# Attention for pairs of query tiles: products of 256 columns, the value matrix applied to the result, rows of scores in 18 places, four gather buffers

## The reference, cut to what matters

```python
x = x + deformable_conv(groupnorm(x), offset_w, offset_b, conv_w)   # 8 images, 128 channels, 56 x 56
t = tokens(x)                                                       # 8 x 3136 x 128
n = layernorm(t)
q, k, v = n @ Wq.T, n @ Wk.T, n @ Wv.T
scores = where(causal, q @ k.T * 128 ** -0.5, -inf)
t = t + softmax(scores) @ v
m = layernorm(t)
probs = softmax(m @ gate_w.T + gate_b, over tokens)                 # 64 experts, top 8 tokens of each
t = t + scatter(experts(gather(m, top 8)), top 8)                   # gelu(pooled @ w1) @ w2 for 64 experts
```

## Time and profile before

| | us |
|---|---|
| median of 3 runs (3008.95 to 3011.6) | 3009.99 |
| the profiled execution | 3008.08 |
| its span, first to last instruction | 3006.3 |
| first part | 0 to 2813 |
| second part | 2813 to 3006 |
| one image in the steady part (1029.6 to 1364.0) | 334.5 |

### The profile page before, as it was taken

One profiled execution on the slowest core, in us unless ns is written; L12 is line 12 of the kernel. 1 busy time (PEld: TensorE's weight loads), 2 busy tenths in 40 slices (PEclk: granted clock), 3 DMA queues, 4 the chain that ended last, 5 costly groups with the idle time before them and its releaser, 6 DMA issues. The chain is left out here.

```text
span 3006.3 us, 52942 instructions
## 1 busy us (share of the span) xinstructions
PE 2696.6 (90%) x18970; PEld 2111.6 (70%) x18970; DVE 1896.5 (63%) x7132; ACT 1775.2 (59%) x4046; POOL 1752.8 (58%) x1813
## 2 busy tenths in 40 slices
PE   5788999999999999999999999999999998999555
PEld 3566776778777777778777776778777886777333
DVE  3566666766587667766587667766586658654314
ACT  2555666666666666666666666666666666664210
POOL 5777775775477656775577647775577657700000
PEclk8899999999999999999999999999999998999677
DMA  7444334633355325532354325532363324320497
GB/s 184 122 142 136 113 107 124 162 113 90 89 154 139 96 80 146 147 113 85 103 151 133 96 77 149 148 112 85 107 174 114 101 81 118 115 94 9 161 347 282
DMA packets 221233, 383.21 MB, mean 127 GB/s; under 512 B 44569, under 2 KB 131545, under 8 KB 220459
## 3 DMA queue, kind: packets, MB, share of 16 engines
q0 software_dynamic: 86400, 236.04, 27.5%
q1 hardware_dynamic: 130411, 128.81, 14.0%
q10 hardware_dynamic: 4160, 14.98, 1.2%
HBM read 317.04 MB, written 62.65 MB: 126 GB/s over the span
## 5 line engine op out<-in xcount | busy, mean ns | idle before, releaser
L521 POOL DMA_INDIRECT shared<-pair_table,idx x1800 | 1741.0, 967 | 882.5 <-issue 525.2
L1107 PE MATMUL bank_o<-vals,prob_t 128*128 128x128 f32 x5200 | 676.3, 277 | 73.3 <-ACT prob_t L566 72.4
L810 DVE CUSTOM_DVE_ANT_0 prob<-bank_r,mask 128x512 f32<-128x512 f32 (+3 forms) x728 | 452.0, 631 | 409.1 <-PE bank_r L1085 407.3
L1107 PEld LDWEIGHTS bank_o<-vals,prob_t 128*128 128x128 f32 x5200 | 622.1, 192 | 105.7 <-ACT prob_t L566 96.3
L566 ACT ACTIVATE prob_t<-bank_r 128x512 f32<-128x512 f32 (+3 forms) x728 | 383.0, 547 | 473.6 <-PE bank_r L1094 472.7
L1085 PE MATMUL bank_r<-keys,qt 128*128 128x512 f32 (+3 forms) x1456 | 633.7, 551 | 0.0
L547 ACT ACTIVATE shared<-shared,wa 128x128 f32<-128x128 f32 x1800 | 561.3, 391 | 38.6 <-DMA shared<-pair_table,idx 38.6
L800 DVE SCALAR_TENSOR_TENSOR shared<-shared,wb 128x128 f32<-128x128 f32 x1800 | 510.8, 347 | 84.8 <-ACT shared L547 83.0
L1074 PE MATMUL bank_r<-convw_t,smp_t 128*128 128x128 f32 x3600 | 485.8, 282 | 31.6 <-ACT smp_t L552 31.6
L1074 PEld LDWEIGHTS bank_r<-convw_t,smp_t 128*128 128x128 f32 x3600 | 449.8, 197 | 90.2 <-ACT smp_t L552 58.0
L1094 PE MATMUL bank_r<-ident,prob 128*128 128x128 f32 x2600 | 383.6, 274 | 1.9 <-ACT prob L639 1.9
(11 more groups left out here) (152 smaller groups left out, 2189.3 us busy)
## 6 DMA issues: line engine op xcount, KB each, us to landing
shared<-in_dram SPq DMA_DIRECT2D x32, 1024.0 KB, 10.0
shared<-pair_table,idx POOLq DMA_INDIRECT x1800
pair_table<-rows_out SPq DMA_DIRECT2D x112, 256.0 KB, 3.1
t<-in_dram SPq DMA_DIRECT2D x48, 256.0 KB, 3.6
t_dram<-t SPq DMA_DIRECT2D x48, 256.0 KB, 2.4
shared<-in_dram SPq DMA_DIRECT2D x7, 1568.0 KB, 14.3
stage<-t_dram SPq DMA_DIRECT2D x8, 832.0 KB, 9.8
pm_dram<-logit SPq DMA_DIRECT2D x8, 800.0 KB, 9.8
```

The lines of the kernel that those rows point to most:

```text
L521: pool.indirect_dma_start(g[t % RING][:, n, :], None, pair_table[b % 2], bass.IndirectOffsetOnAxis(ap=idx[:, b % 2, i * TAPS + n:i * TAPS ...
L810: dve.tensor_tensor_reduce(prob_at(t, k0, w), ring_bank(("score", t, c))[:, 0:w], m, 1.0, NEG, ALU.add, ALU.max, cmax[t % 2][:, c:c + 1]). ...
L1107: last = pe.matmul(attn_ps, prob_t[q % 3][:, n * P:(n + 1) * P], vals[:, slot(tb, at), :], start=(at == 0), stop=(at == ti))
```

## The change

**Pairs.** Attention is done for two query tiles at a time (`pair_tiles`, 13 pairs in an image, the last one of a single tile). The product is the other way round: a block of `vals` is the stationary side and the turned probabilities of both tiles are the moving one, 256 columns (L1238 of the new file); where only the second tile of the pair reaches a block, 128. `bank_o` then holds channels by tokens for the pair.

**The value matrix.** `vals` keeps the normalised tokens. After the last product of a pair DVE copies `bank_o` to `z` (L971, 128 x 256) and PE multiplies it by `wv_t` (`values`, L1249, one product for each tile) into a bank of the six. The odd jobs "vals" are gone. `t2` of both tiles is made in the one step in which the pair is finished (`tiles_done`): DVE's list for that step is the copy to `z`, three score banks, the layer norm for `vals` where due, `t2` and statistics twice, the layer norm for `xf` where due, the convolution's sum.

**Lags.** The exponential stays at 7 (`LAG_E`), the products start at 8 (`LAG_V`) and take two steps, the first half of a pair's pieces in one and the second half in the next (`attending`). The pair is finished one step later. In the rounds the scores now stand ahead of the products. The table of odd jobs, the top 8 (now steps 9 to 12) and the indices (13 to 18) are moved by about a step.

**Places.** `RING` is 4; what the fifth buffer took, and `prob`, make 18 places of 512 scores. A row may lie in one to three runs; then the exponential takes one to three instructions (247 for 200 tiles) and DVE adds the sums. DVE waits with a score for the turning of what lay in its place.

**Second part.** Stage pieces (L1370, L1382) are issued by POOL, behind waits of their own. SP issues w1 of round k + 2 behind `first(k - 2)`, and w2 of round k behind `second(k - 4)`; `first` waits for w1 alone and `second` for w2. Round 3's matrices are loaded at step 208 instead of 201.

```diff
-RING = 5
+RING = 4
-LAG_S, LAG_V, LAG_T = 6, 7, 8
+LAG_S, LAG_E, LAG_V = 6, 7, 8
-LMAX, LEXP, LTOP, LREPLACE, LCHOSEN, POOLED_OUT = 8, 9, 9, 10, 11, 15
-INDEX = (12, 13, 14, 16, 17)
+LMAX, LEXP, LTOP, LREPLACE, LCHOSEN, POOLED_OUT = 9, 10, 10, 11, 12, 16
+INDEX = (13, 14, 15, 17, 18)
+def pieces_of(p):
+    if len(pair_tiles(p)) == 1:
+        return [(k, min(PER, TILES - k)) for k in range(0, TILES, PER)]
+    return [(2 * j, 2) for j in range(p + 1)]
+def attending(step):
+    b, r = divmod(step - LAG_V, TILES)
...
+    return [(PAIRS * b + p, j) for j in (range(n // 2) if h == 0 else range(n // 2, n))]
+def finished(step):
+    b, r = divmod(step - LAG_V - 1, TILES)
+    if not 0 <= b < B or not (r % 2 or r == TILES - 1):
+        return None
+    return PAIRS * b + r // 2
@@ ACT
-                    act.activation(row, row, ACT.Exp, bias=nmax[r][:, 0:1], accum_out=total[r][:, 0:1])
+                    for k, (c0, w) in enumerate(runs):
+                        row = columns(c0, w)
+                        last = act.activation(row, row, ACT.Exp, bias=nmax[v % 2][:, 0:1],
+                                              accum_out=total[:, v % 4, k:k + 1])
-                early = chunks_in(v) >= 4
+                early = len(at) >= 4
@@ DVE
+                if pair is not None:
+                    w = len(pair_tiles(pair % PAIRS)) * P
+                    after(attended, pair + 1)
+                    after(valued, pair)
+                    dve.tensor_copy(z[:, 0:w], bank_o[:, 0:w]).then_inc(z_done, 1)
+                for c in range(min(chunks_in(ts), 3)):
+                    keep_scores(ts, c)
...
+                for h, t in enumerate(tiles_done(step)):
...
+                    after(valued, pair + 1)
...
+                    dve.scalar_tensor_tensor(t2[k % 2][:, j, :], ring_bank(("attn", pair, 0))[:, h * P:(h + 1) * P],
@@ PE
+                def values():
+                    use = ("attn", pair, 0)
+                    after(z_done, pair + 1)
+                    free_ring(use)
+                    for h in range(len(pair_tiles(pair % PAIRS))):
+                        last = pe.matmul(ring_bank(use)[:, h * P:(h + 1) * P], z[:, h * P:(h + 1) * P], wv_t[:],
                 for c in range(min(chunks_in(ts), 3)):
                     scores(c)
+                if pair is not None:
+                    values()
@@ second part, SP
-                if k >= WSLOTS:
-                    sp.wait_ge(second_mm, k - WSLOTS + 1)
-                    load_experts(sp, k, 1, w1, w2, shared, w_in)
+                if WSLOTS <= k + 2 < ROUNDS:
+                    sp.wait_ge(first_mm, k + 2 - WSLOTS + 1)
+                    load_experts(sp, k + 2, 1, w1, w2, shared, w_in)
```

More of the change, by code:

```diff
@@ L165, in ring_order @@
         order += [("score", ts, c) for c in range(min(chunks_in(ts), 3))]
+        if finished(step) is not None:
+            order.append(("attn", finished(step), 0))
         order += [("rows", *k) for k in rows_of(step)]
@@ L450, in _ @@
                 b, s = image_of(step)
-                t = step - LAG_T
-                if 0 <= t < ALL:
+                for t in tiles_done(step):
                     tb, i = image_of(t)
@@ L876, in _ @@
+                for t in [t for t in tiles_done(step) if t % TILES % PER == PER - 1 or t % TILES == TILES - 1]:
                     tb, i = image_of(t)
                     m, k = i % PER + 1, GPI * tb + i // PER
-                    at, first = k % 2 * PER, slot(tb, i - m + 1)
+                    row, first = k % 2 * PER, slot(tb, i - m + 1)
                     after(stats_b, t + 1)
@@ L1001, in fill_misc @@
                         last = pe.transpose(bank_misc[:, k * P:(k + 1) * P], vals[:, at + k, :], ident[:])
[L1002 to L1006 removed]
                 elif what == "query":
                     w = group_size(n) * P
+                    emptied(after, ("keys", b, n))
                     last = pe.matmul(bank_misc[:, 0:w], wqk[:], key_chunk(b, n * CHUNK, w), start=True, stop=True)
@@ L1056, in _ @@
             for step in range(END):
-                ts, v = step - LAG_S, step - LAG_V
+                ts, pair, at = step - LAG_S, finished(step), attending(step)
                 b, i = image_of(step)
```

328 lines of the change are left out of this document (203 added, 125 removed), and 39 rows, old and new, of the table MISC.

## The result

The changed kernel takes 3205.7 us (median of 4 runs, 3205.2 to 3208.0), the kernel before 3009.5 beside it: ratio 1.0652, interval 1.0634 to 1.0671. The forecast was 3183, from 3065 to 3245. The profiled execution has a span of 3204.1 us, 197.8 more than before. It has three parts: the first part of the program became 222 us longer (`first(0)` runs at 3041.7 in place of 2819.7), the rounds of the second 26 us shorter, and the tail behind them 2 us longer.

The account below looks back on a forecast made before the run. PE was taken to bound the kernel, with 17 us idle an image. 3006.3 + 179 (seven images) + 15 (first image) - 1 (end of first part) - 20 (second part) = 3179, 3183 beside the median; range 3065 to 3245.

Parts of the forecast that it names:

- Wide products: PE's 256-column products each replace two narrow ones: 15 us gained in all, 1.9 an image, bounds 0 to 18.
- The list: DVE's longer work in steps 12, 16, 20 and 24 leaves PE waiting: +6.3, +4.1, +4.7 and +3.8 us an image.
- Where the waits show: PE idles about 4 us before step 24's last scores, 4 to 7 before the next samples in steps 12, 16, 20.
- Smaller waits: Waits in steps 1 to 5, 8, 10 and 13, less gains in 11 and 21 to 23: +5.5 us an image.
- Clock: PE runs at half rate after new waits of 4 us and more: +3 us an image, 0 to 7 allowed.
- First image: Only steps 16, 20 and 24 wait, half-rate PE adds 1.5, and 9 blocks leave gather waits: +15 us.
- Four buffers: One gather buffer less costs 0 us, since POOL spends its time behind a full ring.
- Second part: Experts' matrices issued earlier let the rounds' transfers run without pause: 20 us gained, 16 to 30.
- half hidden: Rival: long steps push other steps' waits away, 11 us an image, 3075 us in all (3035 to 3130); chance 0.16.
- the pairs win: Rival: DVE's clump of work is hidden and the kernel gets faster, 2975 us; chance 0.06.
- the clock is dearer: Rival: each wait costs a full slow PE stretch or two, 7 to 10 us an image, 3215 to 3235; chance 0.08.

## Why the prediction was right

Its mechanism held: VectorE's list in steps 12, 16, 20 and 24, and the second part's gain against it. These steps and those behind them hold 19.5 of the 30.6 us by which an image grew. The time was 3205.7 for 3183, inside the range; an image took 365.1 us and not 358 to 361. That the sum came so near is in part luck, since its errors had opposite signs.

- *Wide products*: 15 us said, at 0.2155 us for each instruction. The measured 0.2175 (0.87 / 4) gives 2288 x 0.0045 = 10 us, inside the bounds of 0 to 18. The 17.8 us of the line are not a test of it: busy time counts the last instruction of a group to its end (0.27 or 0.38 us), and the new kernel has fewer groups. The sign given for PE did not come either. Its busy time in an image did not fall: with the norm later, at a clock of 0.99 as before, it is 323.3 us for 317.6. What these 5.7 us are was not sought.
- *The list*: 18.9 said for the four steps with the late samples behind them. Measured +13.9 in the steps and +5.6 in their neighbours, 19.5, and of this 15.8 without the clock (the same eight steps with the waits filled take 119.3 us, before the change 103.5). So the list was put 3 us too high. Step 12 was priced too dear: its additions start at 14.4 us and not at 15.2, and PE is idle for 6.0 us of it, where the working had 8.6 up to the end of the late samples. Elsewhere the sum starts where the working has it: in step 24 at 12.85 us (13.2 said), in step 16 at 12.5 (12.7); in step 20 the additions start at 14.4 (14.7).
- *Where the waits show*: wrong in steps 12, 16 and 20. I named the first samples of the next step, released by L918. PE met its own transposes for `keys` and `xf` first (3.94, 2.10 and 1.40 us). Only the run with the transposes moved has the wait where I put it, and in steps 16 and 20 alone. In step 24 it is as said, 3.31 us before L1211, released by L1023.
- *Smaller waits*: +5.5 said, 3.6 with the wide products' gain taken off. Outside the eight steps above an image grew by 11.1, by 10.9 with the waits filled. (The working had 1.4 us of step 13 in this term; here step 13 is with the list.) This is the term that was mis-sized. Step 7 alone has +6.9, and the working does not have it: I counted the last tile's products as moved, and not as moved into a step that PE bounds (argued from the windows, as said). Steps 8 and 10 were near (+1.5 and +2.3 for +2.1 and +1.5); step 9, +1.6, was missing.
- *Clock*: 3 taken, 0 to 7 allowed, about 4 measured by filling the waits. The 1.7 us in its upper bound is in no row; the row that it stands on gives 1.6. Step 9, which fell to 0.88, has none of the four long waits. That the slow stretches fall partly on time in which PE would wait anyway held: PE's pace lost 7 us an image, the image 4.
- *First image*: +15 said, +10.1 measured (295.9 to 306.0).
- *Four buffers*: 0 said, 0 measured in the kernel before.
- *Second part*: 20 said (16 to 30), 26 measured in the changed kernel and 20.5 in the kernel before. That the kernel gains as much without GpSimd's queue is shown.
- *Rivals*: "half hidden" and "the pairs win" fell with the list's rows without a gap; "the clock is dearer" was the nearer one, with step 7 in the clock's place.

An image then came out 5.1 us over the forecast (+7.3 small waits, +0.9 clock, -3.1 list), seven images 36; less 6 of the second part and 5 of the first image this is the difference of 25 us in the span.

## What to carry over

Before changing what an engine does, write out its list for each step and ask which regular jobs fall into the same step: two layer norms in one step, with the transposes and logits that follow the second, cost this kernel 86 us without any pair, and parting them gave 130 back to the changed one. Count the step behind as well, where +9.5 us stood beside +3.8 with single tiles, and look there for work and waits that the move itself brought: two odd jobs side by side in one bank waited for ACT's copy. A wait is named after the first row that needs the late engine; moving that row moves the wait, and moving the late job inside the same list helps only if what is needed next is that job and not the list's end.

## What the runs showed of the hardware

- 92 useless transposes an image, put into waits of 1.4 to 4 us, lifted the mean clock from 0.946 to 0.965 and saved 34 us of 3206.
- In the changed kernel step 9 runs at 0.88 with no wait of PE above 1.00 us in the two steps before it; in the kernel before it runs at 1.00:

```profile
1245.23 0.30 PE L1140 MATMUL bank_misc<-ident,xf 128*128 128x128 f32 x1 [1.00 <-DVE xf L1014]
1245.90 0.66 PE L1131 MATMUL bank_misc<-ident,vals 128*128 128x128 f32 x4 [0.37 <-ACT xf_t L708]
```

- Behind the wait of 2.39 us in step 5 the kernel before runs at 0.93 and takes 24.90 us. With the norm later it has the same wait there, and 1.00:

```profile
1138.81:1162.12 23.31, 20.92 (x144) 15.20 (x142) 8.99 (x33) 14.52 (x24) 8.52 (x9) 1.00 0.17 52
```

  A wait of this length can go either way, and 1.6 us with it.
- With the second part's stage pieces issued by SP or by GpSimd the kernel takes the same time (2986.9 and 2987.9 us).
